# Regrouping the pairs of attention heads over both halves of the model width in a graph-attention and expert-layer kernel

## The chip, the cores and the metric

The kernel runs on one core of one Trainium2 chip. The metric is the device time of one execution in microseconds (us), lower is better. Single executions of the kernel before took between 772.4 and 778.1 us.

## The reference

The input `x` is 32 batches of 256 rows by 256 columns, with one 256x256 adjacency matrix for all batches. Two layers follow each other, each on the normalised input and added to it:

```
x = x + attention(layernorm(x), adj, Wq, bq, Wk, bk, Wv, bv, Wo, bo)
x = x + experts(layernorm(x), controller, f1, f2)

attention: 8 heads of 32 columns
  scores = q @ k.T / sqrt(32);  scores = where(adj == 0, -inf, scores)
  out    = softmax(scores) @ v;  return out @ Wo.T + bo
experts: groups of 16 rows, 64 (expert, set) slots;
  every slot picks the row of the group with the largest logit, sends it
  through f1 (256 -> 32), relu, f2 (32 -> 256), and adds the result to that row
```

The change touches the attention layer alone.

## The kernel before, in words

All engines run hand-ordered programs that synchronise by counting semaphores. TensorE is `pe`, VectorE is `dve`, ScalarE is `act`, GpSimd is `pool`, and SyncE (`sp`) issues nearly all DMA transfers. Every engine's attention program is a function `batch(b, par, last)`, run for b = 0 and 1, then as a hardware loop over pairs of batches (2 to 27), then for 28 to 31; `par` is b mod 2 and picks one of two buffers. The stages of neighbouring batches are interleaved.

The 8 heads are numbered h = 4 g + j, with g the group of 128 columns (G = 2) and j the head within it (HPG = 4). ScalarE and VectorE split each query and key value into a high and a low part (`save_high`, L886, and `save_low`, L1101) in `parts`. SyncE then copies pieces of `parts` into `stack`, 16 transfers of 128 KB for a batch, four (r = 0 to 3) for each j (`stack_parts`, L344), so that one 128-row product gives the score to nearly full precision. A stack block j holds head j of both groups. For batch 0 alone the four transfers of j = 2 are issued by ScalarE (L929), the other twelve by SyncE.

The heads are worked through in eight slots, two slots to a pair `pr`. `head(slot)` gives the head of a slot: before the change pair 0 is heads 0 and 2, pair 1 heads 1 and 3, pair 2 heads 4 and 6, pair 3 heads 5 and 7, so that the first two pairs are group 0 and the last two group 1. For each pair:

- `scores(b, par, n)` (L569, n = 2 pr + t, t a half of the query rows) makes the scores of both heads in a PSUM bank.
- `maximum(b, n)` (L1113, L1115, VectorE) adds the mask and finds the extremes. `exps(b, n)` (L903, ScalarE) takes the exponentials and their sums.
- `p_transpose(b, h)` (L582, TensorE) transposes slot h. `save_pt` copies it out of PSUM into `PTs[:, h]`: VectorE the even slots (L1126), ScalarE the odd ones (L912). The copies of slots 6 and 7 fall into the next batch.
- `pv(b, par, g)` (L596) multiplies the transposed probabilities of the four heads of group g with the values. It also runs in the next batch, between `q_project(b+1)` (L534) and the next batch's scores 2 to 4.
- `normalise` (L1144, VectorE) divides by the sums once their reciprocals have been spread by DMA (L349). `o_project` (L607) applies Wo, and `residual` (L1153) adds the result.

TensorE's order in a batch b of the middle is: `k_project(b+1)`; scores 0 and 1; transposes 6 and 7 of batch b-1; `q_project(b+1)`; `pv` of batch b-1 for g = 0 and 1; scores 2, 3, 4; transposes 0, 1; `v_project(b+1)` (L556); scores 5, 6, 7; transposes 2, 3; `h_transpose(b+2)` (L527); `o_project(b-1)`; transposes 4, 5. VectorE's order is: maximum 0; slot 6 of batch b-1; maximum 1; two low parts; maximum 2; two low parts; maxima 3 and 4; slot 0; maximum 5; `normalise(b-1)`; slot 2; maxima 6 and 7; residual; slot 4; statistics; reciprocals. In odd batches (while b + 4 < 32) VectorE also takes the statistics and the reciprocal roots of batches b+3 and b+4 (`sums_of`, `step`).

Of the kernel before, what the change touches and what calls it, by code (L numbers as in the profile page):

```python
# [23 lines left out]
def gnn_moe_kernel(nc, x, adj, Wq, bq, Wk, bk, Wv, bv, Wo, bo, controller, f1, f2, out):  # L24
# [49 lines left out]
    with ExitStack() as ctx:  # L74
# [3 lines left out]
        def sem(name):  # L78
            return ctx.enter_context(nc.semaphore(name))
# [109 lines left out]

        stacked = [[sem("stacked00"), sem("stacked01")], [sem("stacked10"), sem("stacked11")]]  # L190
        v_ready, v_saved = sem("v_ready"), sem("v_saved")
# [32 lines left out]
        def in_loop(n):  # L224

            return not isinstance(n, int)
# [20 lines left out]
        def head(slot):  # L247

            pr, half = divmod(slot, 2)
            return pr // 2 * HPG + pr % 2 + 2 * half  # L250

# [5 lines left out]
        def slot_of(h):  # L257

            g, j = divmod(h, HPG)
            return 2 * (2 * g + j % 2) + j // 2  # L260

# [69 lines left out]
        def _(sp):  # L331
# [5 lines left out]
            def stack_parts(b, par):  # L337

                sp.wait_ge(q_saved, b + 1)
                sp.wait_ge(k_saved, b + 1)  # L340
                for j in (0, 2, 1, 3):
                    for r in range(4):
                        if not (isinstance(b, int) and b == 0 and j == 2):
                            sp.dma_start(*stack_rows(par, j, r)).then_inc(stacked[par][j % 2], 16)  # L344
            def spread_rows(b):
# [89 lines left out]
        def _(pool):  # L435
# [9 lines left out]


            pool.wait_ge(bias_done, 1)

# [49 lines left out]
        def _(pe):  # L498
# [61 lines left out]
            def scores(b, par, n):  # L560
                pr, t = divmod(n, 2)
                if pr < 2 and t == 0:
                    pe.wait_ge(stacked[par][pr], 128 * (b // 2 + 1) if isinstance(b, int) else (b - par) * 64 + 128)
                before = n - 3 if n > 2 else (-2, -1, -3)[n]
# [21 lines left out]
            def pv(b, par, g):  # L586
                pe.wait_ge(pt_dve, b * 4 + 2 * g + 2)
                pe.wait_ge(pt_act, b * 4 + 2 * g + 2)
                if g == 0:
# [245 lines left out]
        def _(act):  # L835
# [42 lines left out]
            def save_high(b, par, which, ready, bias, done):  # L878

                act.wait_ge(ready, b + 1)  # L880
                if which == 1 or isinstance(b, int) and b == 0:
                    for h in range(2):
                        if in_loop(b) or b > 1:
                            act.wait_ge(stacked[par][h], 128 * (b // 2) if isinstance(b, int) else (b - par) * 64)
                for g in range(G):
                    last = nc.scalar.activation(parts[:, par, 2 * which, g, :], M[1 - which][:, g * N:g * N + N], ACT.Identity,  # L886
                                                bias=bias[:, g:g + 1])
                last.then_inc(done, 1)
# [19 lines left out]
            def save_pt(b, h):  # L908
                act.wait_ge(pt_ready, b * 8 + h + 1)
                if in_loop(b) or 2 * b + h // 4 - 1 > 0:  # L910
                    act.wait_ge(pv_ready, 2 * b + h // 4 - 1)
                nc.scalar.copy(PTs[:, h, :], PTb[h % 2][:, :]).then_inc(pt_act, 1)  # L912
# [14 lines left out]
            act.wait_ge(k_saved, 1)  # L927
            for r in range(4):
                act.dma_start(*stack_rows(0, 2, r)).then_inc(stacked[0][0], 16)  # L929
            save_v(0, 0)  # L930
# [77 lines left out]
        def _(dve):  # L1008
# [113 lines left out]
            def save_pt(b, h):  # L1122
                dve.wait_ge(pt_ready, b * 8 + h + 1)
                if in_loop(b) or 2 * b + h // 4 - 1 > 0:
                    dve.wait_ge(pv_ready, 2 * b + h // 4 - 1)
                nc.vector.tensor_copy(PTs[:, h, :], PTb[h % 2][:, :]).then_inc(pt_dve, 1)  # L1126
# [260 lines left out]
```

## Time and profile before

| | before |
|---|---|
| median of 3 runs | 774.78 us (772.4 to 778.1) |
| profiled execution, its own time | 772.76 us |
| its span, first to last instruction | 771.0 us |
| TensorE busy | 717.6 us (93%) |
| VectorE, ScalarE busy | 606.3 us (79%), 548.1 us (71%) |
| mean granted TensorE clock | 0.981 of full speed |

The attention layer takes the stretch up to about 517 us of the span and the expert layer the rest. Times of rows are counted from the first instruction. `PE` is a matmul, `PEld` the loading of its weights (which overlaps the matmuls), `DVE`, `ACT`, `POOL` and `SPq` the other engines and queues. L569 is line 569 of the kernel.

### The profile page before, as it was taken

The numbers are of one execution on the slowest core, as the hardware profiler recorded it, in microseconds if no ns is written. First come the engines' busy times: TensorE is split into PE (matmuls) and PEld (weight loads), VectorE is DVE, ScalarE is ACT, GpSimd is POOL, SyncE is SP. The second block draws the span as 40 slices with busy tenths as digits, with TensorE's granted clock in tenths as the row PEclk, the third lists the DMA queues.
The fourth block names the chain that finished last, engine by engine and source line by source line (L and its number), as shares of the span: only waits on it lengthen the run. The fifth ranks groups of instructions, "written<-read, shape, count | busy, mean of one in ns | idle before, by whom it ended". The sixth has DMA issues, their size and how long they took to land.

```text
span 771.0 us, 22490 instructions
## 1 busy us (share of the span) xinstructions
PE 717.6 (93%) x7206; PEld 556.8 (72%) x7206; DVE 606.3 (79%) x2574; ACT 548.1 (71%) x1622; POOL 125.2 (16%) x126
## 2 busy tenths in 40 slices
PE   8899999999999999999999999878999998987936
PEld 7688888888888888878888887756565555654623
DVE  6699999999999999999999998877557656655612
ACT  3788989998899999899988998845454444452400
POOL 1110001000100100010001002637325225200000
PEclk9999999999999999999999999999999999998969
DMA  6776786687777767867876777650599999989999
GB/s 181 161 192 151 176 196 156 165 195 167 171 179 167 189 157 171 194 153 170 194 165 165 163 165 162 173 191 1 220 334 320 390 317 321 373 313 318 361 354 323
DMA packets 121591, 166.01 MB, mean 215 GB/s; under 512 B 15296, under 2 KB 84416, under 8 KB 121280
## 3 DMA queue, kind: packets, MB, share of 16 engines
q1 hardware_dynamic: 119072, 163.44, 75.3%
q10 hardware_dynamic: 2464, 1.84, 1.1%
q8 instruction: 35, 0.57, 0.3%
q14 instruction: 20, 0.16, 0.1%
HBM read 47.78 MB, written 41.94 MB: 116 GB/s over the span
## 4 chain that ended last, share of the span: by engine, by line
PE 69%; DMA 8%; DVE 8%; issue 6%; SPq 6%; ACT 2%; DVEq 1%; POOL 0%; POOLq 0%
PE bank L582 12%; PE bank L534 10%; PE bank L607 7%; PE bank L556 7%; PE bank L569 6%; PE bank L759 6%; PE bank L596 5%; PE bank L738 5%; DMA stage<-scratch 4%; PE bank L727 3%; SPq L344 2%; PE bank L785 2%; SPq L390 2%; DMA scratch<-stage 2%; PE bank L527 2%
## 5 line engine op out<-in xcount | busy, mean ns | idle before, releaser
L903 ACT ACTIVATE Ps<-Ps,nmax 128x256 f32<-128x256 f32 x512 | 254.7, 501 | 20.7 <-DVE nmax L1115 19.5
L1115 DVE CUSTOM_DVE_ANT_0 Ps<-bank,masks 128x256 f32<-128x256 f32 x512 | 195.4, 419 | 15.4 <-issue 15.1
L582 PE MATMUL bank<-ident,Ps 128*128 128x128 f32 x1024 | 134.7, 274 | 3.2 <-ACT Ps L903 0.7
L582 PEld LDWEIGHTS bank<-ident,Ps 128*128 128x128 f32 x1024 | 114.6, 140 | 13.3 <-issue 7.3
L534 PE MATMUL bank<-hT,WT 128*128 128x256 f32 x512 | 121.1, 380 | 0.1
L452 POOL TENSOR_TENSOR X<-X,bob 128x512 f32 (+1 forms) x32 | 41.1, 1285 | 408.2 <-ACT hn L868 388.7
L534 PEld LDWEIGHTS bank<-hT,WT 128*128 128x128 f32 x512 | 92.4, 190 | 10.6 <-issue 0.5
L464 POOL TENSOR_SCALAR h<-X,mv,roots 128x256 f32<-128x256 f32 x64 | 79.4, 1255 | 114.4 <-PE bank L727 81.0
L903 ACT ACTIVATION_READ_ACCUMULATOR Ps<-Ps,nmax 128x1 f32 x512 | 97.7, 191 | 0.0
L569 PE MATMUL bank<-stack 128*128 128x256 f32 x512 | 91.1, 310 | 4.0 <-DMA stack<-parts 3.8
L1126 DVE COPY PTs<-bank 128x512 f32<-128x512 f32 x128 | 87.4, 683 | 0.2
L569 PEld LDWEIGHTS bank<-stack 128*128 128x128 f32 x512 | 71.2, 189 | 21.9 <-issue 7.0
L912 ACT COPY PTs<-bank 128x512 f32<-128x512 f32 x128 | 73.7, 576 | 14.2 <-PE bank L582 14.2
L269 ACT COPY XS<-bank 128x512 f32<-128x512 f32 x64 | 37.8, 590 | 58.2 <-PE bank L727 58.2
L999 ACT COPY stage<-bank 128x512 f32<-128x512 f32 x64 | 37.5, 586 | 43.3 <-PE bank L759 43.3
L886 ACT ACTIVATE parts<-bank,few 128x256 fp32r<-128x256 f32 x128 | 53.1, 465 | 17.6 <-PE bank L534 17.5
L1356 DVE COPY stage<-bank 128x512 f32<-128x512 f32 x64 | 43.9, 691 | 26.8 <-PE bank L759 26.8
L607 PE MATMUL bank<-WT,OT 128*128 128x256 f32 x256 | 61.5, 383 | 2.6 <-DVE OT L1144 2.4
L596 PE MATMUL bank<-PTs,Vs 128*32 128x256 f32 x1024 | 62.1, 382 | 0.1
L556 PE MATMUL bank<-WT,hT 128*128 128x256 f32 x256 | 62.0, 386 | 0.0
L269 DVE COPY XS<-bank 128x512 f32<-128x512 f32 x64 | 44.7, 699 | 21.8 <-PE bank L727 21.3
L1314 DVE TENSOR_TENSOR X<-X,bank 128x512 f32<-128x512 f32 x32 | 22.0, 688 | 48.1 <-PE bank L771 25.9
(91 smaller groups left out, 1004.7 us busy)
## 6 DMA issues: line engine op xcount, KB each, us to landing
stack<-parts SPq DMA_DIRECT2D x508, 128.0 KB, 2.4
scratch<-stage SPq DMA_DIRECT2D x64, 512.0 KB, 4.2
stage<-scratch SPq DMA_DIRECT2D x96, 256.0 KB, 4.4
X<-in_x SPq DMA_DIRECT2D x32, 256.0 KB, 2.9
rbc<-turned SPq DMA_DIRECT2D x128, 64.0 KB, 2.1
out<-X SPq DMA_DIRECT2D x32, 256.0 KB, 4.3
XRlast<-scratch SPq DMA_DIRECT2D x16, 512.0 KB, 8.7
f1s<-in_L_ffn_f SPq DMA_DIRECT2D x1, 2048.0 KB, 7.9
```

The lines of the kernel that those rows point to most:

```text
L269: return copy(XS[:, :, :, first:first + 4].rearrange("p k e (j two) -> p k e j two", two=2), banks[:, 4 + 2 * hf:6 + 2 * hf, 0:2 * P].rear ...
L464: last = nc.gpsimd.tensor_scalar(h2[n % NORMS][:, t, :], xtile(tile), mv2[:, tile, 0:1], roots[:, 1, tile:tile + 1], ALU.subtract, ALU.mult)
L534: last = nc.tensor.matmul(m[:, g * N:g * N + N], WT[:, w, k, g * P:g * P + P], hT[:, k, :], start=(k == 0), stop=(k == KT - 1))
L556: last = nc.tensor.matmul(M[0][:, t * D:t * D + D], hT[:, k, t * P:t * P + P], WT[:, 2, k, :], start=(k == 0), stop=(k == KT - 1))
L569: last = nc.tensor.matmul(s_bank(n)[:, h * N:h * N + N], stack[:, par, j, 0, g * N + t * P:g * N + t * P + P], stack[:, par, j, 1, g * N:g ...
L582: last = nc.tensor.transpose(PTb[h % 2][:, k * N + t * P:k * N + t * P + P], Ps[:, pr % 2, t, h % 2, k * P:k * P + P], ident[:, :])
L596: last = nc.tensor.matmul(Ob[32 * j:32 * j + 32, g * N:g * N + N], Vs[:, par, k, h * DH:h * DH + DH], PTs[:, slot_of(h), k * N:k * N + N], ...
L607: done = nc.tensor.matmul(M[1][:, t * D:t * D + D], OT[:, g, t * P:t * P + P], WT[:, 3, g, :], start=(g == 0), stop=(g == G - 1))
L903: last = nc.scalar.activation(Ps[:, pr % 2, t, h, :], Ps[:, pr % 2, t, h, :], ACT.Exp, bias=nmax[:, pr % 2, t, h:h + 1], scale=-1.0, accum ...
L912: nc.scalar.copy(PTs[:, h, :], PTb[h % 2][:, :]).then_inc(pt_act, 1)
L1115: last = nc.vector.tensor_tensor_reduce(out=Ps[:, pr % 2, t, h, :], in0=s_bank(n)[:, h * N:h * N + N], in1=masks[:, t, :], scale=1.0, scal ...
L1126: nc.vector.tensor_copy(PTs[:, h, :], PTb[h % 2][:, :]).then_inc(pt_dve, 1)
```

## The change

A pair becomes head j of both groups (heads j and j+4), so pair `pr` reads stack block j = pr alone. Every stack block and parity has a semaphore of its own, counting four transfers instead of eight, and TensorE waits for one block ahead of each pair. SyncE issues the blocks in the order 0, 1, 2, 3. For batch 0, SyncE issues j = 0 (r = 0, 1), 1 and 3, ScalarE j = 0 (r = 2, 3), and GpSimd j = 2 on a semaphore `first_stack`. Group 0 now has the even slots and group 1 the odd ones, so `pv(b, par, 0)` waits for all four copies of VectorE, the one of slot 6 included, and `pv(b, par, 1)` for all four of ScalarE. `save_high` for k waits for four semaphores where it waited for two.

```diff
-        stacked = [[sem("stacked00"), sem("stacked01")], [sem("stacked10"), sem("stacked11")]]
+        stacked = [[sem(f"stacked{par}{j}") for j in range(HPG)] for par in range(2)]
+        first_stack = sem("first_stack")
 def head(slot):
-            pr, half = divmod(slot, 2)
-            return pr // 2 * HPG + pr % 2 + 2 * half
+            return slot % 2 * HPG + slot // 2
 def slot_of(h):
-            return 2 * (2 * g + j % 2) + j // 2
+            return 2 * j + g
+        def stack_landed(b, par, j):
+            if isinstance(b, int) and b == 0 and j == 2:
+                return first_stack, 64
+            apart = 64 if par == 0 and j == 2 else 0
+            return stacked[par][j], (64 * (b // 2 + 1) if isinstance(b, int) else (b - par) * 32 + 64) - apart
 stack_parts, SyncE:
-                for j in (0, 2, 1, 3):
+                for j in range(HPG):
                     for r in range(4):
-                        if not (isinstance(b, int) and b == 0 and j == 2):
-                            sp.dma_start(*stack_rows(par, j, r)).then_inc(stacked[par][j % 2], 16)
+                        if not (isinstance(b, int) and b == 0 and (j == 0 and r > 1 or j == 2)):
+                            sp.dma_start(*stack_rows(par, j, r)).then_inc(stacked[par][j], 16)
 GpSimd, ahead of its wait for bias_done:
+            pool.wait_ge(q_saved, 1)
+            pool.wait_ge(k_saved, 1)
+            for r in range(4):
+                nc.gpsimd.dma_start(*stack_rows(0, 2, r)).then_inc(first_stack, 16)
 scores, TensorE:
-                if pr < 2 and t == 0:
-                    pe.wait_ge(stacked[par][pr], 128 * (b // 2 + 1) if isinstance(b, int) else (b - par) * 64 + 128)
+                if t == 0:
+                    pe.wait_ge(*stack_landed(b, par, pr))
 pv, TensorE:
-                pe.wait_ge(pt_dve, b * 4 + 2 * g + 2)
-                pe.wait_ge(pt_act, b * 4 + 2 * g + 2)
+                pe.wait_ge((pt_dve, pt_act)[g], b * 4 + 4)
 save_high, ScalarE:
-                    for h in range(2):
+                    for j in range(HPG):
                         if in_loop(b) or b > 1:
-                            act.wait_ge(stacked[par][h], 128 * (b // 2) if isinstance(b, int) else (b - par) * 64)
+                            act.wait_ge(*stack_landed(b - 2, par, j))
 save_pt, ScalarE and VectorE alike:
-                if in_loop(b) or 2 * b + h // 4 - 1 > 0:
-                    act.wait_ge(pv_ready, 2 * b + h // 4 - 1)
+                if in_loop(b) or 2 * b + h % 2 - 1 > 0:
+                    act.wait_ge(pv_ready, 2 * b + h % 2 - 1)
 ScalarE, ahead of the first batch:
-            for r in range(4):
-                act.dma_start(*stack_rows(0, 2, r)).then_inc(stacked[0][0], 16)
+            for r in (2, 3):
+                act.dma_start(*stack_rows(0, 0, r)).then_inc(stacked[0][0], 16)
```

## Rows read from the trace of the kernel before

**Rows 1.** By stretch: PE, PEld, DVE, ACT, POOL busy; PEclk, DMA share, GB/s.

```profile
34.00:500.00 466.00, 461.42 (x3568) 388.85 (x3567) 431.45 (x2162) 419.05 (x1353) 52.48 (x43) 1.00 0.73 172
```

**Rows 2.** Waits, whole span: us in total, times, longest.

```profile
PE bank L569 <- DMA stack<-parts: 3.8, 4, 1.9
```

**Rows 3.** Timeline of batch 0, TensorE and ScalarE: start, us, what, idle before.

```profile
24.42 0.54 PEld L569 LDWEIGHTS bank<-stack 128*128 128x128 f32 x4 [1.06 <-DMA stack<-parts]
24.54 1.08 ACT L868 ACTIVATE hn<-X,shift,root 128x256 f32<-128x256 f32 x2
25.78 0.51 ACT L903 ACTIVATE Ps<-Ps,nmax 128x256 f32<-128x256 f32 x1 [0.16 <-DVE nmax L1115]
...
28.55 0.19 ACT L903 ACTIVATION_READ_ACCUMULATOR Ps<-Ps,nmax 128x1 f32 x1
28.78 0.78 PEld L569 LDWEIGHTS bank<-stack 128*128 128x128 f32 x6 [2.29 <-DMA stack<-parts]
...
29.50 0.90 PEld L582 LDWEIGHTS bank<-ident,Ps 128*128 128x128 f32 x8
...
30.14 0.51 ACT L903 ACTIVATE Ps<-Ps,nmax 128x256 f32<-128x256 f32 x1 [1.39 <-DVE nmax L1115]
```

**Rows 4.** Stack transfers of batch 0: issues, DMA share, and issue to landing.

```profile
16.65 2.67 ACTq L929 DMA_DIRECT2D stack<-parts  x4
...
24.42 16.75 SPq L344 DMA_DIRECT2D stack<-parts  x17
...
22.00:23.00 1.00, 1.00 (x6) 0.87 (x6) 0.40 (x1) 0.00 (x0) 0.51 (x1) 1.00 1.07 199
...
stack<-parts SPq DMA_DIRECT2D x1, 128.0 KB, 4.3
```

**Rows 5.** Timeline of batch 18 (even), TensorE and VectorE.

```profile
298.14 0.69 DVE L1126 COPY PTs<-bank 128x512 f32<-128x512 f32 x1
298.65 1.45 PEld L596 LDWEIGHTS bank<-PTs,Vs 128*32 128x32 f32 x32 [0.33 <-issue]
...
300.51 0.77 PEld L569 LDWEIGHTS bank<-stack 128*128 128x128 f32 x6 [0.41 <-issue]
301.06 0.42 DVE L1115 CUSTOM_DVE_ANT_0 Ps<-bank,masks 128x256 f32<-128x256 f32 x1 [0.75 <-issue]
...
301.49 0.86 PEld L582 LDWEIGHTS bank<-ident,Ps 128*128 128x128 f32 x8 [0.21 <-issue]
...
305.29 0.69 DVE L1144 TENSOR_TENSOR OT<-bank,rbc 128x512 f32<-128x512 f32 x1
...
306.07 1.60 PEld L607 LDWEIGHTS bank<-WT,OT 128*128 128x128 f32 x8
```

**Rows 6.** Timeline of batch 19 (odd), ScalarE, VectorE and TensorE.

```profile
312.05 0.59 ACT L912 COPY PTs<-bank 128x512 f32<-128x512 f32 x1 [0.36 <-PE bank L582]
312.26 0.69 DVE L1126 COPY PTs<-bank 128x512 f32<-128x512 f32 x1
...
313.67 0.37 PEld L596 LDWEIGHTS bank<-PTs,Vs 128*32 128x32 f32 x12 [0.33 <-issue]
```

**Rows 7.** Stack transfers of batch 19 and the first score that reads them.

```profile
302.65 10.39 SPq L344 DMA_DIRECT2D stack<-parts  x16
...
310.29 0.64 PEld L569 LDWEIGHTS bank<-stack 128*128 128x128 f32 x4
```

**Rows 8.** Timeline of the last batch, 31.

```profile
491.13 0.53 PEld L569 LDWEIGHTS bank<-stack 128*128 128x128 f32 x4 [1.05 <-DMA stack<-parts]
...
493.34 0.42 DVE L1115 CUSTOM_DVE_ANT_0 Ps<-bank,masks 128x256 f32<-128x256 f32 x1
...
494.03 0.69 DVE L1126 COPY PTs<-bank 128x512 f32<-128x512 f32 x1
...
494.77 0.59 PEld L596 LDWEIGHTS bank<-PTs,Vs 128*32 128x32 f32 x16 [0.62 <-DVE PTs L1126]
...
496.31 0.78 PEld L569 LDWEIGHTS bank<-stack 128*128 128x128 f32 x6 [0.95 <-DMA stack<-parts]
```

More of the change, by code:

```diff
@@ L1123, in save_pt @@
                 dve.wait_ge(pt_ready, b * 8 + h + 1)
-                if in_loop(b) or 2 * b + h // 4 - 1 > 0:
-                    dve.wait_ge(pv_ready, 2 * b + h // 4 - 1)
+                if in_loop(b) or 2 * b + h % 2 - 1 > 0:
+                    dve.wait_ge(pv_ready, 2 * b + h % 2 - 1)
                 nc.vector.tensor_copy(PTs[:, h, :], PTb[h % 2][:, :]).then_inc(pt_dve, 1)
```

## The prediction

> **What bounds the kernel now.** I read the busy times of the whole span first (the small table: TensorE 93%), then the same by stretch. In the middle of the attention layer TensorE is busy 461.4 of 466 us, at the full clock [rows 1], so two things can move the time: TensorE's idle places, and work that starts to hold TensorE up. The list of waits shows how little the first can be: TensorE waits for a stack transfer four times in the whole span, 3.8 us together [rows 2]. Then the timeline, batch by batch. Two of the four waits lie in batch 0 [rows 3], two in batch 31 [rows 8]. In the thirty batches between there is none, and that is no accident of a single row: the 16 issues of a batch take 10.39 us, 0.65 each, the eighth begins 7 x 0.65 after 302.65, at 307.2, and lands 2.4 later (the page's median from issue to landing), at 309.6, while the first score loads at 310.29 [rows 7].
>
> **Batch 0: the stack arrives earlier.** Before, pair 0 needs eight transfers and pair 1 all sixteen. Weight loading stands still 1.06 us ahead of the first score and 2.29 ahead of score 2 [rows 3]. The last SyncE issue is at 24.42 and takes 4.3 us to land, which gives 28.72, just ahead of the load at 28.78 [rows 3, 4]. After, pair 0 needs four transfers, issued by two queues in two steps. Scaled by bytes, they go out among about six of the sixteen: the sixteen occupy the DMA engines from some 17.8 to 27 us, and the share of 1.07 at 22 to 23 us says that they are full [rows 4]. Six sixteenths of 9.2 us is 3.4, plus some 1.7 us to land: 22.9, ahead of TensorE, which would be there at 24.42 - 1.06 = 23.36. So the first stall goes. Pair 1 needs twelve sixteenths: 17.8 + 6.9 + 1.7 = 26.4, where TensorE would want it at 28.78 - 2.29 - 1.06 = 25.43. The second stall shrinks from 2.29 to about 1.0.
>
> What is late next? The transposes of pair 0 (L582 at 29.50) need the exponentials 0 and 1, and ScalarE has its own queue: the normalisation for batch 2 keeps it until 24.54 + 1.08 = 25.62, and the first exponential starts at 25.78, 0.16 later. So it can start only about 0.1 earlier; the second is done at 28.55 + 0.19 - 0.1 = 28.6, and the transposes can load at about 28.75 instead of 29.50 (0.13 after ScalarE, as elsewhere). That is 0.75. Exponential 2, at 30.14 after an idle 1.39, then starts up to 1.4 earlier, but its slot copy waits for those transposes, and from there ScalarE is busy on and on until TensorE waits for it at 35.2. I take **-1.0 us** for batch 0, with -3.3 (both stalls, if nothing follows) and +0.3 as ends.
>
> The four issues moved to GpSimd have no row. ScalarE's four took 2.67 us, 0.67 each [rows 4]; the upper bound from GpSimd's own rows is one of its arithmetic instructions, 1.285 us. Between them, the last is issued at 16.65 + 5.1 = 21.8 at the latest and lands by 26.1. Block 2 is first read by score 4, at about 26.6, and the transposes behind it cannot start before 28.75: covered by 2 us. Behind these issues GpSimd has only the bias addition of batch 0, whose bias is ready at 22.4. If the cover failed, the start would gain nothing.
>
> The full DMA share says how much a third issuer can bring: nothing but an earlier issue [rows 4]. The Trainium skill says the same as a rule (DMA: Bandwidth & Descriptors, "Issuing engines are not separate DMA queues"): all issuers feed the same 16 engines, and issuing from several of them saves only sequencer time. By the rule alone pair 3's block would come no earlier than 28, and the sum above stays as it is, since score 6 wants it only three microseconds after score 2. For an issue from GpSimd the same page ("Anatomy of one DMA") gives 2.0 us plus bytes over 436 GB/s, an estimate of 2.3 us for 128 KB unloaded; no row here shows it.
>
> **Batches 1 to 30: earlier blocks bring nothing, the new wait of the P·V product costs.** The stack waits are already met, so finer ones gain 0. TensorE has two stack waits more and two copy waits fewer in a batch: 0. ScalarE's two additional waits stand before the high part of k; the slot copy behind it still idles 0.36 us for TensorE in batch 19 [rows 6], which hides them. The moved waits of `save_pt` are met, since the transposes come after `pv` on TensorE.
>
> But `pv` for group 0 now waits for VectorE's copy of slot 6, which it didn't need. In batch 19 that copy ends at 312.26 + 0.69 = 312.95 and `pv` starts at 313.67: 0.72 to spare [rows 6]. In batch 18 it ends at 298.83, and `pv` starts at 298.65, 0.18 before it [rows 5]. VectorE is late in even batches because the odd batch before carries the statistics and root steps of two later batches. I went through all: in 11 even batches (6 to 26) the copy ends 0.17 to 0.20 after the start of `pv`, in batch 30 0.22 after, in batch 4 0.02 before, in 2 and 28 0.2 before, in the odd ones 0.7 or more before. TensorE starts some 0.05 us after a VectorE end (494.03 + 0.69 = 494.72, load at 494.77) [rows 8]. So `pv` starts 0.23 later in an even batch, and so do scores 2 to 4.
>
> Is that hidden? The transposes of slots 0 and 1 stand 0.21 us after the loads of those scores [rows 5], as they wait for ScalarE: that takes up 0.21 of the 0.23. VectorE's path doesn't. Maximum 2 starts 0.55 after score 2 (301.06), and from there VectorE has no gap up to `normalise`, whose end, 305.29 + 0.69 = 305.98, lets `o_project` load at 306.07 [rows 5]. With 0.23 more it loads at 306.26, **0.19 later**, and behind it TensorE has no gap. VectorE's following work waits for TensorE, so each even batch pays anew: 11 x 0.19 = 2.1, batch 30 0.25, batch 4 0.03, together **+2.4 us** (ends: 0 if VectorE catches up, 3.5 at 0.27 in 13 batches).
>
> **Batch 31.** Score 0 idles 1.05 us for the eighth transfer [rows 8]; four land 4 x 0.65 earlier, so that goes. But maximum 0 starts at 493.34 because VectorE is busy until then, and slot 6 is copied by 494.72 as before. `pv`, whose first half now runs before that, would start both halves at 494.77 and take 1.86 (a batch's 32 matmuls in the chain of waits): score 2 at 496.63, not 496.31. TensorE is then 0.32 later, of which the 0.21 us wait of the next transposes takes most: **+0.1** (ends -0.8 and +0.4).
>
> **Sum.** -1.0 + 2.4 + 0.1 = +1.5 us. Against the profiled execution (772.76, its span plus 1.8) that is 774.3; that run lies 2.0 under the median of 774.78, so on the median it is **776.3**. The expert layer is unchanged.
>
> **The rivals.** (a) Start and end give all they can, and VectorE makes up for the wait: -3.3 - 0.8 + 0 = -4.1, **770.7**. For it: the idle rows add up to 3.35 in batch 0. Against it: ScalarE's unbroken work. (b) Slower: the copy of slot 6 holds `pv` in every batch. Point from which: VectorE 0.7 us later in the odd batches than now. At 0.28 us (0.23 and a wait's latency again) for 31 batches, 8.7 - 1.0 = 7.7, **782.5**. Against it: the 0.72 to spare. (c) The change doesn't do what it says at the start: GpSimd's transfers come after 29 us and pair 2 takes over the stall of pair 1: 0 + 2.5 = **777.3**. For it: no row of GpSimd issuing exists. (d) The new wait is hidden but ScalarE limits the start: -0.9, **773.9**.
>
> **How the numbers follow.** Forecast 0.50, (a) 0.14, (b) 0.07, (c) 0.12, (d) 0.17. About 1%, 7.7 us, is what a measurement here can tell from no change. Only (b) touches it, at its edge, and (a) could with a run-to-run shift: faster 0.03, same 0.91, slower 0.06. The range runs from (a) to past the sum of the upper ends (+0.3 + 3.5 + 0.4 = 4.2, 779.0), with the 2 to 3 us by which single runs stray: 770.5 to 781.0.
>
> **What would show it.** In the profile after: no DMA idle before the first L569, a first L582 load near 28.75; in even batches L596 loads 0.23 later against the end of L1126, released by it; L607 released by L1144; two batches 30.4 us apart instead of 30.2; one DMA wait at most in batch 31. Wrong I would be if L607 keeps its place (then (d)), if the first transposes come at 26 to 27 (then (a)), or if L569 waits for a stack transfer ahead of score 4.

## The result, and the profile after

The changed kernel takes **772.87 us** (median of 20 runs, 768.82 to 774.66); the kernel before, run beside it, 774.87 (20 runs, 772.4 to 779.95). The ratio is 0.9964, with a 95% interval of 0.9947 to 0.9981: 0.4% faster, where +1.5 us was forecast. The time lies in the predicted range; the sign was wrong. The profiled execution took 772.04, its span 770.2.

In the file after, the line numbers have moved: `scores` L580, `p_transpose` L593, `pv` L606, `o_project` L617, VectorE's slot copy L1136, ScalarE's L922, the exponentials L913.

By stretch, the row that answers to [rows 1]:

```profile
34.00:500.00 466.00, 459.56 (x3562) 388.71 (x3562) 429.23 (x2155) 416.07 (x1345) 52.50 (x43) 1.00 0.73 171
```

TensorE is 1.9 us less busy in the same 466 us. The list of waits says where it now stands. The row of [rows 2] is no longer in it, and TensorE has a new row, the wait of the P·V product for VectorE's slot copy, as a matmul and as a weight load:

```profile
PE bank L606 <- DVE PTs L1136: 3.9, 14, 1.6
PEld bank L606 <- DVE PTs L1136: 10.4, 17, 1.9
```

Batch 0 in the timeline (start, us, what, idle before it), against [rows 3] and [rows 4]:

```profile
16.37 1.33 ACTq L939 DMA_DIRECT2D stack<-parts  x2
...
17.01 2.35 POOL L457 DMA_DIRECT2D stack<-parts  x4 [14.05 <-DVE parts L1111]
...
23.38 0.64 PEld L580 LDWEIGHTS bank<-stack 128*128 128x128 f32 x4
...
25.51 0.50 ACT L913 ACTIVATE Ps<-Ps,nmax 128x256 f32<-128x256 f32 x1
25.58 0.88 PEld L580 LDWEIGHTS bank<-stack 128*128 128x128 f32 x6
...
28.34 0.86 PEld L593 LDWEIGHTS bank<-ident,Ps 128*128 128x128 f32 x8 [1.89 <-ACT Ps L913]
```

Score 0 loads at 23.38 without a wait, and score 2 at 25.58 without one too. The transposes then wait for ScalarE. GpSimd's issues took 2.35 / 4 = 0.59 each.

Batch 18 (even), against [rows 5]:

```profile
297.51 0.69 DVE L1136 COPY PTs<-bank 128x512 f32<-128x512 f32 x1
298.25 1.45 PEld L606 LDWEIGHTS bank<-PTs,Vs 128*32 128x32 f32 x32 [0.57 <-DVE PTs L1136]
...
300.86 0.87 PEld L593 LDWEIGHTS bank<-ident,Ps 128*128 128x128 f32 x8
...
304.84 0.69 DVE L1154 TENSOR_TENSOR OT<-bank,rbc 128x512 f32<-128x512 f32 x1
...
305.58 1.59 PEld L617 LDWEIGHTS bank<-WT,OT 128*128 128x128 f32 x8
```

`pv` loads 0.05 after the copy's end (298.20) and names it as what it waited for. The 0.21 us that stood before the transposes is gone: the delay fills it. From the copy's end to the load of `o_project` it is 7.38 us; before it was 306.07 - 298.83 = 7.24 [rows 5].

Batch 31, against [rows 8]:

```profile
490.37 0.54 PEld L580 LDWEIGHTS bank<-stack 128*128 128x128 f32 x4
...
494.10 0.68 DVE L1136 COPY PTs<-bank 128x512 f32<-128x512 f32 x1
...
494.84 1.45 PEld L606 LDWEIGHTS bank<-PTs,Vs 128*32 128x32 f32 x32 [1.88 <-DVE PTs L1136]
...
496.70 0.77 PEld L580 LDWEIGHTS bank<-stack 128*128 128x128 f32 x6 [0.41 <-issue]
```

No stack transfer is waited for; `pv` runs in one piece, and score 2 loads 1.86 behind it.

**Where the time goes, from several profiles.** The attention layer ends for TensorE with the last `pv` (the matmuls of batch 31). I read five marks in each profile: the first score of batches 1, 3, 27 and 30, and that last `pv`.

| profile | batch 1 | 3 | 27 | 30 | last `pv` | 3 to 27 | 30 to last `pv` |
|---|---|---|---|---|---|---|---|
| before, shown ahead | 38.20 | 68.50 | 431.13 | 476.64 | 509.11 | 362.63 | 32.47 |
| before_again | 40.16 | 70.51 | 433.18 | 478.73 | 513.09 | 362.67 | 34.36 |
| look_before | 39.89 | 70.22 | 433.29 | 478.82 | 511.04 | 363.07 | 32.22 |
| look_before_2 | 39.81 | 70.13 | 432.69 | 478.22 | 512.81 | 362.56 | 34.59 |
| look_before_3 | 38.06 | 68.59 | 431.58 | 477.10 | 510.29 | 362.99 | 33.19 |
| after | 36.80 | 67.05 | 431.17 | 476.69 | 509.26 | 364.12 | 32.57 |
| after_again | 36.79 | 67.04 | 431.10 | 476.63 | 509.16 | 364.06 | 32.53 |
| after_third | 36.81 | 67.07 | 431.14 | 476.65 | 509.19 | 364.07 | 32.54 |

The kernel before ends its attention anywhere from 509.11 to 513.09, the changed one at 509.2 in each of its three. The profile on which I forecast ended earliest of the five. Against it the change gives -1.40 (up to batch 1) + 1.45 (batches 1 to 30) + 0.10 (the rest) = +0.15 us; against the mean of the five (39.22, 477.90, 511.27) it gives -2.42 + 1.18 - 0.83 = -2.07, beside a difference of the medians of 2.00. That the two agree to 0.1 is partly luck: the five ends scatter with a standard error of some 0.8 us. What follows the last `pv` takes 261.5 us on the mean of the five before and 261.3 on that of the three after. The means show no part of the expert layer in the gain, but single executions differ there by 4 us, so a part of one microsecond would not be seen.

### The profile page after: what moved, and what is told of

Same layout as the page of the kernel before. It is cut to its first block, busy times and chain, and to the rows that moved or that the text cites. A ratio compares the mean times of both kernels' runs of the same rounds, so it can differ in the third digit from the quotient of the medians.

```text
span 770.2 us, 22457 instructions
## 1 busy us (share of the span) xinstructions
PE 712.3 (92%) x7206; PEld 554.9 (72%) x7206; DVE 605.7 (79%) x2574; ACT 546.5 (71%) x1622; POOL 127.6 (17%) x130
## 4 chain that ended last, share of the span: by engine, by line
PE 47%; DVE 22%; issue 14%; DMA 8%; SPq 3%; ACT 3%; DVEq 2%; POOL 0%; POOLq 0%
PE bank L593 7%; PE bank L769 6%; DMA stage<-scratch 5%; PE bank L748 5%; PE bank L606 4%; PE bank L617 4%; PE bank L567 4%; PE bank L580 4%; DVE Ps L1125 4%; DVE PTs L1136 3%; PE bank L737 3%; PE bank L545 3%; SPq L397 2%; DVE nmax L1125 2%; DVE stats L1066 2%
## 5 line engine op out<-in xcount | busy, mean ns | idle before, releaser
L913 ACT ACTIVATE Ps<-Ps,nmax 128x256 f32<-128x256 f32 x512 | 254.7, 501 | 22.7 <-DVE nmax L1125 21.4
L593 PE MATMUL bank<-ident,Ps 128*128 128x128 f32 x1024 | 134.8, 274 | 5.1 <-ACT Ps L913 2.6
L593 PEld LDWEIGHTS bank<-ident,Ps 128*128 128x128 f32 x1024 | 114.2, 140 | 13.9 <-issue 5.3
L545 PEld LDWEIGHTS bank<-hT,WT 128*128 128x128 f32 x512 | 92.4, 190 | 10.8 <-ACT Vs L886 0.8
L913 ACT ACTIVATION_READ_ACCUMULATOR Ps<-Ps,nmax 128x1 f32 x512 | 97.5, 191 | 0.0
L580 PE MATMUL bank<-stack 128*128 128x256 f32 x512 | 91.4, 311 | 0.0
L1136 DVE COPY PTs<-bank 128x512 f32<-128x512 f32 x128 | 87.6, 684 | 0.2
L580 PEld LDWEIGHTS bank<-stack 128*128 128x128 f32 x512 | 71.6, 189 | 16.4 <-issue 7.8
L922 ACT COPY PTs<-bank 128x512 f32<-128x512 f32 x128 | 73.7, 576 | 11.2 <-PE bank L593 11.2
L606 PE MATMUL bank<-PTs,Vs 128*32 128x256 f32 x1024 | 61.9, 382 | 3.9 <-DVE PTs L1136 3.9
L617 PE MATMUL bank<-WT,OT 128*128 128x256 f32 x256 | 61.8, 384 | 2.8 <-DVE OT L1154 2.6
```

Source lines behind the costliest of these rows:

```text
L545: last = nc.tensor.matmul(m[:, g * N:g * N + N], WT[:, w, k, g * P:g * P + P], hT[:, k, :], start=(k == 0), stop=(k == KT - 1))
L580: last = nc.tensor.matmul(s_bank(n)[:, h * N:h * N + N], stack[:, par, j, 0, g * N + t * P:g * N + t * P + P], stack[:, par, j, 1, g * N:g ...
L593: last = nc.tensor.transpose(PTb[h % 2][:, k * N + t * P:k * N + t * P + P], Ps[:, pr % 2, t, h % 2, k * P:k * P + P], ident[:, :])
L606: last = nc.tensor.matmul(Ob[32 * j:32 * j + 32, g * N:g * N + N], Vs[:, par, k, h * DH:h * DH + DH], PTs[:, slot_of(h), k * N:k * N + N], ...
L617: done = nc.tensor.matmul(M[1][:, t * D:t * D + D], OT[:, g, t * P:t * P + P], WT[:, 3, g, :], start=(g == 0), stop=(g == G - 1))
L913: last = nc.scalar.activation(Ps[:, pr % 2, t, h, :], Ps[:, pr % 2, t, h, :], ACT.Exp, bias=nmax[:, pr % 2, t, h:h + 1], scale=-1.0, accum ...
```

## The experiments

Each was run beside the kernel before on the same chip; ratios have 95% intervals, and "batch 1", "3 to 27" and "last `pv`" are the marks of the table.

### 1. Both kernels again, and the kernel before once more by itself

The unchanged files, as `before_again`, `after_again`, `after_third`, and single looks `look_before`, `look_before_2`, `look_before_3`.

> The kernel before against itself. Theory 1 (the attention layer is even in the two profiles, +0.15 us at its end, so the measured -2.0 us of the medians comes from the expert layer: TensorE's clock fell twice more in the profiled execution of before, at 543 and at 706 us): ratio 1.000 with the measurement's own scatter of some 0.2%, and clock dips of 3 to 7 us length near 543 or 706 us in some profiles of this kernel. Rival (the difference of the medians is scatter between runs): a ratio as far from 1 as 0.996 to 1.004.

> The changed kernel once more. Theory 1: ratio 0.996 to 0.998 again, the attention layer ends within 0.3 us of the last profile's, and no clock dip near 543 us. Rival (scatter): ratio 0.999 to 1.001.

> The changed kernel a third time, on this chip. Theory: ratio 0.996 to 0.999, batch 1 at 36.8 us and the end of the attention layer at 509.2 as in both profiles so far, since its stalls are gone and with them what varies. Rival: a profile with a clock drop at 30 us or a late batch 31.

> A third profile of the kernel before, to see how its stalls vary. Theory (the stalls and the clock behind them vary from run to run): score 0 of batch 1 lies at 38.2 without a clock drop and near 40 with one, and batch 31 takes 14.5 us to its first score without and 15.9 with a late transfer. Rival: it repeats the first profile.

> A further profile of the kernel before, to count. Four of the five profiles with the start of before had a clock drop at about 30 us, and two of five a first score of batch 31 over 15.5 us behind that of batch 30. Theory: a drop here too, batch 3 at 70.2. Rival: as the first profile, 68.5.

> One more profile of the kernel before, for the same count as look_before_2. Theory: a clock drop at about 30 us and batch 3 at 70.2. Rival: as the first profile, no drop and batch 3 at 68.5.

Before_again: 773.83 (12 runs), 1.0002 [0.9984, 1.002]. After_again: 773.40 (12), 0.9989 [0.9968, 1.001]. After_third: 771.77 (12), 0.9970 [0.9948, 0.9992]. Looks: 776.40, 775.30, 774.23. Over all 44 runs of the changed kernel the median is 772.37, over all 145 of the one before 773.81: 1.4 us, or 0.2%. Against the runs beside it the changed kernel was 2.0, 0.4 and 1.7 us faster. The gain is small and real; one comparison alone (after_again) does not show it, and came out as its rival had it. Theory 1 of before_again, that the gain lies in the expert layer, is not borne out by the marks.

Batch 0 in the trace of before_again, with the stretches that follow (PE, PEld, DVE, ACT, POOL busy; PEclk; DMA share; GB/s):

```profile
29.25 0.78 PEld L569 LDWEIGHTS bank<-stack 128*128 128x128 f32 x6 [2.85 <-DMA stack<-parts]
29.97 1.32 PEld L582 LDWEIGHTS bank<-ident,Ps 128*128 128x128 f32 x8
```

```profile
29.00:30.00 1.00, 0.74 (x6) 0.75 (x7) 0.20 (x2) 0.00 (x0) 0.00 (x0) 1.00 0.00 0
30.00:31.00 1.00, 1.00 (x8) 1.00 (x8) 1.00 (x6) 0.39 (x1) 0.00 (x0) 0.69 0.00 0
31.00:32.00 1.00, 1.00 (x6) 0.91 (x5) 1.00 (x7) 0.98 (x5) 0.00 (x0) 0.50 0.00 0
32.00:33.00 1.00, 1.00 (x4) 0.82 (x3) 1.00 (x8) 1.00 (x4) 0.00 (x0) 0.50 0.37 80
33.00:34.00 1.00, 1.00 (x4) 0.79 (x4) 0.36 (x1) 0.31 (x2) 0.00 (x0) 0.60 0.88 195
```

The stall ahead of score 2 is 2.85 us here instead of 2.29, and about a microsecond behind it the granted clock falls to 0.50, the lower of the two levels (1.2 GHz), for some 3.4 us; the eight transposes take 1.32 instead of 0.90. Summed over the stretches, the missing clock is 0.31 + 0.50 + 0.50 + 0.40 = 1.7 us. From the load of score 2 to batch 1 it takes 40.16 - 29.25 = 10.91 us here and 38.20 - 28.78 = 9.42 in the profile shown ahead, so the fall cost 1.5 us there. It does so wherever it appears: of seven profiles of kernels with the start of before (these five, wait_alone, wait_last), five show the fall at 28 to 34 us and take 10.8 to 10.9 from that load to batch 1, and the two without it, the first one shown ahead and look_before_3, take 9.42. None of the three profiles of the changed kernel shows a fall there.

Batch 31 of before_again: the score, and its sixteen stack transfers (issue ns min/median/max; us to landing min/median/max):

```profile
494.67 0.93 PEld L569 LDWEIGHTS bank<-stack 128*128 128x128 f32 x4 [2.50 <-DMA stack<-parts]
```

```profile
L344 SPq DMA_DIRECT2D stack<-parts x16: 594/601/1408, 486.2 to 496.7; - x16
...
DMA to landing us min/median/max: 2.3/2.4/3.9
```

What the DMA queues carried from 491 to 494 us (packets, MB, share of the 16 engines):

```profile
q8 instruction: 1, 0.02, 2.0%
```

One issue took 1.41 us instead of 0.60, and one transfer 3.9 us to land instead of 2.4. It was among the eight that score 0 needs: 2.50 us of stall instead of the 1.05 of [rows 8], and the clock fell to 0.50 behind it (495 to 498). Look_before_2 (issue 2.01, landing 4.1, stall 2.79) shows the same, look_before_3 (1.53, 3.4, stall 1.95) a smaller form without the fall. The traces show what comes together with it. The queue that the profile calls `instruction` carries 35 packets of 16 KB in the whole execution. One of them starts within 0.1 us of the beginning of the long issue, in these three profiles (492.1, 491.6, 487.9) and in the three others that have a long issue in batch 31 (wait_alone 493.5, both runs of swap_groups 485.8). In the profile shown ahead it starts at 483.4, ahead of the first issue of the batch at 484.1, and in the three profiles of the changed kernel at 483.5 or 483.6; none of these has a late transfer in that batch. That the load of instructions holds up the issue is the likely reading; no run moved it on purpose.

### 2. The wait for slot 6 taken out of the changed kernel (swap_groups, swap_groups_2)

```
- return slot % 2 * HPG + slot // 2            # head(slot)
+ return (1 - slot % 2) * HPG + slot // 2
- return 2 * j + g                             # slot_of(h)
+ return 2 * j + 1 - g
- pe.wait_ge((pt_dve, pt_act)[g], b * 4 + 4)
+ pe.wait_ge((pt_act, pt_dve)[g], b * 4 + 4)
```

Group 0 now lies in the slots that ScalarE copies, and the waits of `save_pt` on `pv_ready` are turned to match.

> The changed kernel with the groups' slots exchanged: group 0 in the odd slots, copied by ScalarE, group 1 in the even ones, copied by VectorE. The first P.V product then waits for ScalarE's copy of slot 7, which ends 1.1 us before it, and VectorE's copy of slot 6 is needed 0.93 us later. Theory: the wait on slot 6 costs 0.12 to 0.15 us for every pair of batches (measured: 30.34 us for two batches after, 30.20 before), so two batches come back to 30.20 and the attention layer ends 1.5 to 1.9 us earlier than after; the ratio to before falls by another 0.002. Rival (something else in the regrouping stretches the pairs of batches, for instance the additional waits): two batches stay at 30.34 us.

> swap_groups once more, beside the changed kernel on the same chip. Theory: 1.6 us below the changed kernel in the attention layer, so a ratio of 0.995 to 0.997 against before. Rival: what swap_groups gained was scatter, ratio as the changed kernel's.

Swap_groups: 769.46 (12 runs), 0.9957 [0.9938, 0.9976]. Swap_groups_2: 771.50 (12), 0.9976 [0.9949, 1.0003], a little above the 0.995 to 0.997 of its theory. The changed kernel beside them took 773.40 and 771.77, so the medians put the changed kernel 3.9 us behind on one chip and 0.3 on the other; the marks are steadier. The last `pv` starts at 507.43 and 507.41, 1.8 earlier than in the changed kernel; 3 to 27 takes 362.4. Batch 18:

```profile
296.49 0.69 DVE L1136 COPY PTs<-bank 128x512 f32<-128x512 f32 x1
296.99 1.45 PEld L606 LDWEIGHTS bank<-PTs,Vs 128*32 128x32 f32 x32 [0.33 <-issue]
...
303.63 0.68 DVE L1154 TENSOR_TENSOR OT<-bank,rbc 128x512 f32<-128x512 f32 x1
304.42 1.60 PEld L617 LDWEIGHTS bank<-WT,OT 128*128 128x128 f32 x8
```

`pv` again starts 0.19 before the copy of slot 6 ends (297.18), and `o_project` is back at 7.24 from it. So the wait costs 364.08 - 362.4 = 1.7 us in batches 3 to 27. The start keeps its gain (batch 1 at 36.83). Its batch 31 shows the other half: one issue took 1.40 us and one landing 3.5 (in the second run 1.84 and 4.0), and no score waited. So the new pairs do pass a late transfer by.

```profile
L351 SPq DMA_DIRECT2D stack<-parts x16: 593/604/1401, 482.5 to 493.0; - x16
```

### 3. The wait put alone into the kernel before (wait_alone, wait_last)

In `pv`, for both groups; the two kernels differ only in the order of the two waits:

```
  pe.wait_ge(pt_dve, b * 4 + 4)               # wait_alone: ahead of pt_act, instead of 2 * g + 2
```

```
  pe.wait_ge(pt_act, b * 4 + 2 * g + 2)
  pe.wait_ge(pt_dve, b * 4 + 4)               # wait_last: behind pt_act
```

> The kernel before with one edit: the P.V product of group 0 waits for VectorE's copy of slot 6 too. Theory: two batches take 30.34 us instead of 30.20 from batch 6 on, so the attention layer ends 1.5 to 2.4 us later than before, and the ratio is 1.002 to 1.003. Rival (the wait is hidden): no change in the spacing, ratio 1.000.

> wait_alone with its two waits exchanged, so that the late one, on VectorE's slot 6, is the last ahead of the P.V matmuls and the one on ScalarE stands before it. In wait_alone P.V starts 0.23 us after the copy's end and a pair of batches takes 30.56 us; in the changed kernel, with one wait, 0.05 us after it and 30.34. Theory (a wait that stands in an instruction of its own adds 0.2 us once it is the late one): P.V starts 0.05 after the copy, a pair takes 30.34, the ratio falls from 1.007 to 1.002. Rival (the regrouping itself shortens the pair, the form of the wait is nothing): 30.56 us again.

Wait_alone: 779.31 (6 runs), 1.0073 [1.0051, 1.0096], 3 to 27 takes 366.68. Wait_last: 776.19 (12), 1.0035 [1.0008, 1.0061], 364.00. Against the mean of before (362.78) that is +3.9 and +1.2. The ratio of wait_alone rose over twice as far as its theory said (1.0073 instead of 1.002 to 1.003); only wait_last reproduces the step of the changed kernel (364.08). The trace shows why. The P·V product of batch 5, which runs in batch 6, in wait_alone and then in wait_last:

```profile
119.10 0.69 DVE L1126 COPY PTs<-bank 128x512 f32<-128x512 f32 x1
...
120.02 1.93 PE L596 MATMUL bank<-PTs,Vs 128*32 128x256 f32 x32 [0.36 <-DVE PTs L1126]
```

```profile
118.60 0.69 DVE L1126 COPY PTs<-bank 128x512 f32<-128x512 f32 x1
...
119.34 1.93 PE L596 MATMUL bank<-PTs,Vs 128*32 128x256 f32 x32 [0.17 <-DVE PTs L1126]
```

The copy ends at 119.79 and `pv` starts 0.23 later; in wait_last it is 0.05. What TensorE's queue does between the copy's end and `pv` (119.0 to 120.3), in wait_alone alone:

```profile
L588 PEldq ALU_OP  x1: 32/32/32, 119.8 to 119.8; - x1
```

```profile
L592 PEldq EVENT_SEMAPHORE  x1: 51/51/51, 119.9 to 119.9; - x1
```

The register operation of the next wait (L588) and the wait for `v_saved` (L592) stand behind the late one and run only when it has been met; in wait_last neither row lies in that stretch. The two rows account for 83 ns of the 180 by which the starts differ; the rest has no row.

### 4. The two halves of the start, apart (three_issuers_old_pairs, two_issuers)

Three_issuers_old_pairs keeps the old pairs and their waits (eight transfers for pair 0, four of them now counted by `first_stack`) and changes only who issues in batch 0:

```
- if not (isinstance(b, int) and b == 0 and j == 2):
+ if not (isinstance(b, int) and b == 0 and (j == 0 and r > 1 or j == 2)):
+ nc.gpsimd.dma_start(*stack_rows(0, 2, r)).then_inc(first_stack, 16)    # r in 0..3, on POOL
- for r in range(4): act.dma_start(*stack_rows(0, 2, r))
+ for r in (2, 3):   act.dma_start(*stack_rows(0, 0, r))
```

Two_issuers is the changed kernel with its new pairs and semaphores, but ScalarE issues block 2 as before and GpSimd nothing.

> The kernel before with only the issuing of batch 0's transfers changed: SyncE, ScalarE and GpSimd as in the changed kernel, the pairs and their waits as before. Theory: the DMA engines are full there, so pair 1 still waits for all sixteen transfers and score 2 of batch 0 stays at 28.5 to 29.3 us; ratio 0.999 to 1.001. Rival (the three issuers are what brings the start): score 2 comes at 27 us or earlier.

> The changed kernel with the issuing of before: SyncE all but j = 2, ScalarE the four of j = 2, GpSimd none. Theory: the regrouping brings nearly all of the start; score 0 of batch 0 loads at 23.4 to 23.9 us, score 2 within 1 us of the changed kernel's 25.6, and the transposes of pair 0 at 28.3 to 28.5 as they wait for ScalarE anyway; ratio within 0.001 of the changed kernel's. Rival (three issuers needed): score 2 at 27 us or later, and batch 1 over 0.5 us later than in the changed kernel.

Three_issuers_old_pairs: 770.83 (12), 0.9961 [0.9939, 0.9984]; batch 1 at 36.83, batch 3 at 67.75, 3 to 27 in 362.56, last `pv` at 508.10. Two_issuers: 772.34 (12), 0.9987 [0.9963, 1.0011]; 37.17, 67.43, 364.08, 509.59. Batch 0 of the first, then of the second:

```profile
27.40 0.77 PEld L576 LDWEIGHTS bank<-stack 128*128 128x128 f32 x6 [1.92 <-DMA stack<-parts]
28.12 0.89 PEld L589 LDWEIGHTS bank<-ident,Ps 128*128 128x128 f32 x8
```

```profile
27.14 0.77 PEld L576 LDWEIGHTS bank<-stack 128*128 128x128 f32 x6 [0.73 <-DMA stack<-parts]
28.71 0.86 PEld L589 LDWEIGHTS bank<-ident,Ps 128*128 128x128 f32 x8 [0.80 <-ACT Ps L909]
```

With the old pairs, score 2 needs all sixteen transfers, and it loads at 27.40, not at 28.6 to 29.3: three issuers bring the last block 1.2 to 1.9 us forward, which was its rival and not its theory. In two_issuers score 2 loads at 27.14, 1.6 us behind the changed kernel, where its theory had 1 at most. Either half alone brings nearly the whole start, since ScalarE's work without a gap sets it from there: 36.83 and 37.17 against 36.80 with both. The halves are not equal afterwards. The old pairs still wait past batch 0 (in this profile 0.30 us in batch 2, and weight loading stands 1.04 and 1.33 us ahead of the first two pairs of batch 31); in none of the six profiles of kernels with the new ones does a score of a later batch wait for its stack, but those with the wait for slot 6 pay 364.08 - 362.56 = 1.5 us in batches 3 to 27.

What does the third issuer do? In three_issuers_old_pairs the last of the sixteen is issued at 24.82, 0.4 us later than before (24.42), and lands at 27.36 instead of 28.74: it takes 2.5 us instead of 4.3. So it is not the time of issuing that is saved. The DMA queues from 15 to 30 us (packets, MB, share of the 16 engines), ScalarE's four transfers in the kernel before, then GpSimd's four in three_issuers_old_pairs:

```profile
q10 hardware_dynamic: 288, 0.52, 15.4%
```

```profile
q0 software_dynamic: 192, 0.52, 11.3%
```

The same 0.52 MB go in fewer and larger packets from GpSimd's queue and occupy the DMA engines a quarter less. Over all queues, 2.3 MB take 67.9% of the engines' time in that stretch before and 59.5% here. Two_issuers, without GpSimd, ends its sixteen transfers at 28.68, as late as before.

### 5. Did the fall of the clock make the difference? (keep_warm, keep_warm_short, warm_start, look_warm)

The kernel before, with dummy matmuls that fill the stalls, written to a PSUM bank that nothing uses at the time.

```
+ if first: keep_busy(18)              # ahead of score 2 of batch 0; short: 9; warm_start: 9
+ if last:                             # ahead of the first score of batch 31; not in warm_start
+     pe.wait_ge(v_saved, B)
+     keep_busy(16, M[0])              # short: 6
```

> The kernel before with dummy matmuls on TensorE in its two idle places: 18 ahead of score 2 of batch 0 and 16 ahead of score 0 of batch 31 (0.11 us each, into free PSUM banks). No wait is changed. Theory (clock): the stalls for the stack cost the kernel before more than their length, because the granted clock falls to half for some 3.5 us behind the longer ones (seen behind 2.3 us of idle in batch 0 and behind 2.3 in batch 31 of the second profile of before, not in the first); busy, TensorE keeps the full clock there, and the median comes 1 to 2.5 us below before, ratio 0.997 to 0.999, near that of the change. Rival (length only): the stalls are as long, so the ratio is 1.000 or a little over.

> keep_warm with the dummies cut to what fits in the stalls: 9 in batch 0 and 6 in batch 31. In keep_warm a dummy took 0.22 to 0.23 us (two passes), so 18 and 16 of them held TensorE 1.2 to 3 us beyond the stack's arrival; there was no clock drop at 30 or 495 us all the same. Theory (clock): no drop in batches 0 and 31, score 2 of batch 0 at 28.7 to 29.3, batch 1 at 38.2 to 38.4 in every run, median 1 to 2.5 us below before (0.997 to 0.999). Rival (the drops do not matter to the end): ratio 1.000 or above.

> The kernel before with nine dummy matmuls ahead of score 2 of batch 0 alone. Theory (the clock drop behind that stall is 1.7 of the 3 us by which the changed kernel starts batch 3 earlier): no drop at 30 us, batch 1 at 38.2, median 0.5 to 1.7 us below before, ratio 0.998 to 0.999. Rival (what the clock gives there is lost again at the next late stack transfer, as keep_warm_short's profile had it, or the drop is not what costs): ratio 1.000 to 1.001.

> A second profile of keep_warm_short. Theory: no clock drop at 30 or at 495 us again. Open is whether batch 3 comes at 68.5, as without a late stack transfer, or at 69.6, as in its first profile, where transfers for batches 1 and 2 were late.

| kernel | median (n) | ratio | batch 1 | last `pv` |
|---|---|---|---|---|
| keep_warm | 778.82 (12) | 1.0072 [1.004, 1.0104] | 39.84 | 515.1 |
| keep_warm_short | 774.73 (12) | 1.0011 [0.999, 1.0032] | 38.15 | 510.12 |
| warm_start | 775.01 (12) | 1.0019 [0.9999, 1.004] | 38.72 | 509.75 |
| look_warm (keep_warm_short again) | 772.57 (1) | | 39.59 | 510.71 |

The dummies of keep_warm, in its batch 0:

```profile
26.29 4.20 PEld L504 LDWEIGHTS bank<-ident 128*128 128x128 f32 x36
...
30.41 0.77 PEld L569 LDWEIGHTS bank<-stack 128*128 128x128 f32 x6
```

Eighteen of them are 36 rows in the trace and took 0.23 us each, so they outlasted the stall and score 2 loads at 30.41: this kernel lost by my sizing. The shorter ones end in time. No fall at 28 to 34 shows in three of the four profiles. In look_warm score 0 had already stood 2.63 us, the clock fell at 25.4 behind it, and it was still at 0.50 when the dummies began at 27.36:

```profile
27.00:28.00 1.00, 1.00 (x5) 0.82 (x3) 0.11 (x1) 0.00 (x0) 0.00 (x0) 0.50 0.03 8
```

In all four, batch 1 comes 9.42 or 9.43 us behind the load of score 2 (keep_warm_short 38.15 - 28.73), as in the two profiles of before without a fall: behind score 2 the dummies do take the 1.5 us of the clock away. Yet no median came down, as the rivals had it. The traces show a reason in the next batch. In all four profiles, and in none of the fourteen others, the last stack transfers of batch 1 are late (issue 1.28 to 1.64 us, landing 3.2 to 3.7), in three of them with the `instruction` packet inside the long issue (40.5 to 41.9 us). Score 2 of that batch then stands 0.73 to 1.10 us, where 0.41 is usual. In keep_warm_short what the dummies saved by batch 1 (38.15) was gone by batch 3 (69.60, the mean of before being 69.59). So these kernels trade one loss for another, and how much of the medians' gain is the clock is not shown by their medians.

## Why the prediction was wrong

**Score 0 of batch 0: right.** Forecast at 23.36, measured 23.38, no stall.

**Score 2 of batch 0: wrong, without effect on the sum.** The forecast had it wait for pair 1's block until 26.4. It loads at 25.58 with no wait in two profiles of after and at 25.90 with 0.35 in the third. I had read the full DMA share as "nothing but an earlier issue", and that reading failed. The stretch from 21 to 22 us, then that from 26 to 27, each before and after (the last three numbers are PEclk, DMA share and GB/s):

```profile
21.00:22.00 1.00, 0.87 (x4) 0.48 (x4) 0.58 (x3) 0.66 (x2) 0.00 (x0) 1.00 1.03 201
21.00:22.00 1.00, 0.61 (x3) 0.24 (x2) 0.70 (x2) 0.65 (x2) 0.00 (x0) 1.00 1.04 316
```

```profile
26.00:27.00 1.00, 0.90 (x5) 0.44 (x3) 1.00 (x6) 0.94 (x5) 1.00 (x1) 1.00 0.90 191
```

```profile
26.00:27.00 1.00, 0.67 (x6) 0.46 (x4) 1.00 (x6) 1.00 (x6) 1.00 (x1) 1.00 0.08 20
```

At the same full share 201 GB/s moved before and 316 after, so a full share did not fix how much moves. The last of the sixteen transfers lands at 26.84 (27.50 and 27.21 in the other profiles of after) instead of 28.74, though in two of the three it was issued later than before (24.96 and 24.68 against 24.42). The rule of the Trainium skill that stood here (DMA: Bandwidth & Descriptors, "Issuing engines are not separate DMA queues") is that several issuers save only sequencer time. The measurement differs: experiment 4 shows that the last issue was no earlier, and that GpSimd's transfers occupied the DMA engines a quarter less for the same bytes. By the reading that I hung on the rule, pair 3's block no earlier than 28, there was nothing to gain either. The estimate for one GpSimd transfer by the same page of the Trainium skill ("Anatomy of one DMA", 2.3 us unloaded) has no row here; under this load those four took 4.4 us at the median, by the table of DMA issues:

```profile
stack<-parts POOLq DMA_DIRECT2D x4, 128.0 KB, 4.4
```

**ScalarE sets the start then: right.** Transposes forecast at 28.75, measured 28.34, waiting for an exponential. Term forecast -1.0, measured -1.40 against the same profile. The first exponential started at 25.51, 0.27 earlier and not 0.1, since neighbouring ScalarE rows overlap by 0.1 and 25.62 was no lower bound; and the chain of the first four exponentials ran in 2.79 us instead of 2.96. Rival (a) needed 26 to 27.

**GpSimd's issues: faster than both bounds.** Between 0.67 and 1.285 forecast, 0.59 measured; the cover of block 2 held, and rival (c) did not occur.

**The new wait: right in kind, too dear.** `pv` names VectorE's copy, 0.05 behind it, in the even batches; swap_groups takes the cost away and wait_last adds it alone. Forecast 0.19 for an even batch and +2.1 up to batch 30. Measured 0.14 (7.38 against 7.24), and +1.45 between batches 1 and 30; two batches are 30.34 us apart, not 30.4. Of the 0.18 by which `normalise` is later, some 0.04 goes into the gap between its end and `o_project`'s load, which shrinks from 0.09 to 0.05 (batch 18). Rival (d) fell with that, and (b) too: odd batches do not wait.

**Batches 30 and 31: small, as forecast, against the same profile.** Forecast 0.25 + 0.1 = +0.35, measured +0.10.

**The step that failed: "Batch 31" and "Batch 0" price the stalls that the change takes away at the length of one execution** (1.06, 2.29 and 1.05 us). In that execution no stack transfer was late and the clock did not fall. In others the same places cost up to 2.86 us ahead of score 2 and 2.79 ahead of batch 31, and the fall of the clock behind the first cost another 1.5 us in three of the five profiles. The changed kernel showed 0.35 us of stall in one of its three profiles, and nothing of the rest. Against the profile that I read, the terms sum to +0.15 where +1.5 was forecast: 1.4 us of the error lie in the size of the start (0.4), of the wait (0.7) and of the end (0.25). The other 2.2 us, and the sign, lie in what that profile didn't show. Against the mean of the five, 1.0 of them is in batch 0 (three falls in five profiles, 0.9, and a score 2 that loads 0.14 later), 0.3 in batches 1 to 30, and 0.9 in the last two batches, where three of the five had a late transfer. I had put the 2.0 us by which that profile lay under the median into the level of both kernels, and most of it belonged to the part that the change removes.

That both events, the late transfer and the fall of the clock, are behind the spread is read from the rows of the profiles, and the shares rest on five of them. That their removal alone makes a kernel's median lower was not isolated: the dummies of experiment 5 brought a late transfer of their own. In the end part luck may help the changed kernel: its three profiles had no late transfer in batch 31 at all, and only swap_groups shows that such a one is passed by.

**A version that beats both:** swap_groups, whose last `pv` is at 507.4, 3.9 us before the mean of the kernel before and 1.8 before the changed one. Its gain over the changed kernel is shown by these marks; of the two pairs of medians one shows 3.9 us and the other 0.3. Three_issuers_old_pairs, which has no new wait, has a median of 770.83 and its last `pv` at 508.10, but ran on another chip than either run of swap_groups; which of the two is better stays open.

## What to carry to other kernels

A stall on a transfer has a spread of its own: before pricing one, read several profiles, ask what happens if a single issue or landing is 1.5 us late, and count what stands behind it. Look in the DMA queues for a packet of instructions at that moment. A change that gives slack there can be worth more than the stall of one profile, as here, and a single profiled execution 2 us under the median should be asked which stalls it was spared. When two buffers are filled by two engines, give the product that comes first the buffers of the engine that is early: here that is the swap of two group numbers, worth 1.7 us. A DMA share of 1.0 is busy time and not a rate: read the GB/s beside it. And of several waits ahead of an instruction, write the one that will be met last behind the others.

## What was not expected of the hardware

- **The order of waits counts.** A late wait with a register operation (32 ns) and another wait (51 ns) behind it let the matmul start 0.23 us after the release; with nothing behind it, 0.05. In batches 3 to 27 that made +3.9 against +1.2 us.
- **The clock falls in some executions of the same program and not in others.** Behind stalls of 2.66 to 2.86 us ahead of score 2 it fell to 0.50 in four of four profiles, behind 2.28 and 2.29 in none of two; wait_last had 2.21 there after 2.40 ahead of score 0, and it fell. Behind score 0 alone it fell after 2.63 (look_warm) and not after 2.35 (keep_warm_short). Each fall behind score 2 took 1.7 us of clock and cost 1.5 us of time.
- **A stack transfer is now and then late**: issue 1.4 to 2.0 us instead of 0.60, landing 3.4 to 4.1 instead of 2.4. In all six profiles where this happens in batch 31, a 16 KB packet of the `instruction` queue starts within 0.1 us of the beginning of the long issue.
- **GpSimd's transfers occupied the DMA engines less.** The same 0.52 MB took 192 packets and 11.3% of the stretch from 15 to 30 us, ScalarE's 288 and 15.4%.
- **A transfer of 128 KB is issued by GpSimd in 0.59 us**, no slower than by SyncE (0.60).
